# Maximum pass of attention as 64-row matmul pairs on the two halves of TensorE's array, two pairs issued together

## Chip, cores and metric

The kernel runs on one core of a Trainium2 chip. The metric is the device time of one execution in microseconds (us): the median over runs. Engines are named as in the profile: PE (TensorE matmuls), PEld (its weight loads), DVE (VectorE), ACT (ScalarE), POOL (GpSimd) and SP (SyncE, which issues the transfers).

## What is computed

Four stages over x of 4 batches x 1024 positions x 256 features, each on the layer-normed x and added to it: a linear recurrent block, a sparse feed-forward block, attention, and the feed-forward block again. The change touches attention alone, where there are 8 heads of 64 and keys and values that come from one 64-wide latent:

```python
q = (x @ Wq.T).reshape(b, t, N_HEADS, HEAD_DIM)
kv_latent = x @ Wkv_down.T
k = (kv_latent @ Wk_up.T).reshape(b, t, N_HEADS, HEAD_DIM)
v = (kv_latent @ Wv_up.T).reshape(b, t, N_HEADS, HEAD_DIM)
scores = jnp.einsum('bqhd,bkhd->bhqk', q, k) * HEAD_DIM ** (-0.5)
attn = jax.nn.softmax(scores, axis=-1)
out = jnp.einsum('bhqk,bkhd->bqhd', attn, v)
return out.reshape(b, t, N_HEADS * HEAD_DIM) @ Wo.T
```

## The kernel before

The key projection is folded into the query, so that keys are the 64-wide latent for all heads. Work is split into 64 **items** W: batch B = W // 16, then head and half c of the 1024 queries, so an item is one head with 512 queries against 1024 keys. Numbers of 64 rows are kept as two f16 parts, high and low. In `kA` rows 0 to 63 hold the high part of the keys and rows 64 to 127 the low part, `qA` holds the high part of the queries in both halves of its rows, `kB` and `qB` the rest, so that two 128-row matmuls give an accurate score tile.

Each item has 8 **steps** kt, one for each 128 keys. On PE step kt of item W issues, in this order:

- at even steps a **pair of the maximum pass** for item W + 2, `max_scores(W + 2, j)` with j = kt / 2 (pairs 0 to 3): 128 of the item's 512 queries, taken with a stride of 4 (`every[:, j, :]`), against both halves of the keys, two matmuls of 128x512 (L1734) into the PSUM banks 2 (j % 2) and 2 (j % 2) + 1
- the **score tile** `scores(W, kt)`: two matmuls (L1746, L1748) into bank 6 or 7, which wait until ACT has done the exponential of the tile two before
- at steps 3, 4, 6 and 7 a quarter of `weighted(W - 1, .)`, 24 matmuls with 64 or 65 columns (L1763 to L1765)
- **side work** in two slots, the first at steps 0 and 1, the second at step 5: queries (L1673), keys (L1666), latent (L1680), transposes (L1659, L1689) and the output product (L1696) of this batch and its neighbours, by tables that name item and slot (`QUERY_AT`, `OUT_FINAL_AT` and others). All of it uses bank 4, and each piece first waits until the piece before has been read out of the bank.

DVE reduces each maximum pair (L1397, 128x1024 from two PSUM banks to one column). Pair j may be issued when the reduction of pair j - 2 is done, by `wait_from(pe, a_mx, W * MX + j - 1)`. DVE's queue holds, per item: reduction 0, low half of tile 0 (L1414), reduction 1, side work (L1381 is the low part of queries), reduction 2, low half of tile 4, reduction 3, and the division of the item before (L1406, L1408). POOL makes the low halves of the other six tiles (L673). ACT does for each tile the exponential (L1007) and, behind the next tile's exponential, its f16 high half (L1015), and copies of side work (L988, L993); DVE's and POOL's low halves wait for the high half. The four maxima go, scaled (L1000), by a small transfer of SP into a row of `qB`, long before the item's score tiles want them. Every engine's order is fixed by these loops.

Of the kernel before, what the change touches and what calls it, by code (L numbers as in the profile page):

```python
# [7 lines left out]
F16 = mybir.dt.float16  # L8
BF16 = mybir.dt.bfloat16
ALU = mybir.AluOpType  # L10
ACT = mybir.ActivationFunctionType
X = mybir.AxisListType.X

P = 128
# [3 lines left out]
CH = 512  # L18
# [6 lines left out]
HD = 64  # L25
# [20 lines left out]
def hybrid_block_kernel(nc, x_in, W_in, b_in, params_log, W_mid, b_mid, w1_w, w1_b, w2_w, w2_b,  # L46
# [4 lines left out]
    with ctx:  # L51
# [3 lines left out]
        def sem(name):  # L55
            return ctx.enter_context(nc.semaphore(name))
# [47 lines left out]
        def carve(shape, dt=F32, parts=P):  # L104
            n = 1
            for s in shape:
                n *= s
            words = n if dt == F32 else (n + 1) // 2
            a = arena[0:parts, room[0]:room[0] + words]
            room[0] += words  # L110
            assert room[0] <= ARENA, room[0]
            if dt != F32:
                a = a.bitcast(dt)
            if len(shape) == 2:
                a = a.rearrange("p (a b) -> p a b", a=shape[0])
            if len(shape) == 3:
                a = a.rearrange("p (a b c) -> p a b c", a=shape[0], b=shape[1])
            return a
# [71 lines left out]
        kB_words = arena[:, room[0]:room[0] + TIME]  # L190
        kB = [carve([TIME], F16) for _ in range(2)]
        kA = [carve([TIME], F16) for _ in range(2)]
        latR = [carve([TIME // P, HD + 1], F16) for _ in range(2)]
        latL = [carve([TIME // P, HD], F16) for _ in range(2)]
        mx = [carve([TPC]) for _ in range(2)]
# [26 lines left out]
        ps = [psum[:, i, :] for i in range(8)]  # L222
# [78 lines left out]
        a_k = sem("a_key_high")  # L301
# [35 lines left out]
        ALL = BATCH * ITEMS  # L337
# [28 lines left out]
        def place(W):  # L366

            B, w = W // ITEMS, W % ITEMS
            hh, c = w // 2, w % 2
            return B, hh, c, hh % Q_RING  # L370

        def query_done(W):

            B, hh, c, slot = place(W)
            return ((B * GROUPS + hh // 2) * 2 + c) * 2 + hh % 2 + 1
# [15 lines left out]
        def wait_from(engine, sem_, value):  # L391

            if value > 0:
                engine.wait_ge(sem_, value)
# [319 lines left out]
        def _(act):  # L714
# [258 lines left out]
            def keys(B, c, bank):  # L973
                cs = slice(c * CH, c * CH + CH)
                act.wait_ge(a_kps, B * 2 + c + 1)
                nc.scalar.activation(kA[B % 2][:, cs], ps[bank][:, :], ACT.Copy).then_inc(a_k, 1)
                nc.scalar.activation(kB[B % 2][0:HD, cs], ps[bank][0:HD, :], ACT.Copy).then_inc(a_k, 1)

            def latent(B, c, bank):
                act.wait_ge(a_lps, B * 2 + c + 1)  # L980
# [41 lines left out]
            for c in range(2):  # L1022
                keys(0, c, 4 + c)
# [8 lines left out]
            for W in range(ALL):  # L1032
                B, w = W // ITEMS, W % ITEMS
# [426 lines left out]
        def _(pe):  # L1460
            mm = nc.tensor.matmul
# [83 lines left out]
            for a in range(NH // 2):  # L1545
                o = bank_for(4 + a)
                for k in range(KB2):
                    last = nc.tensor.transpose(o[:, k * P:k * P + P], wo_n[:, k, a * P:a * P + P], ident[:, :])
                last.then_inc(s_pe0, 1)
            for a in range(NH // 2):  # L1550
                o = bank_for(8 + a)
                pe.wait_ge(s_ev0, 5 + a)
                for r in (0, HD):
                    last = mm(o[r:r + HD, 0:D], wv_n[r:r + HD, a, :], woT[r:r + HD, a, :], start=True, stop=True)
                last.then_inc(s_pe0, 1)
            for k in range(KB2):
                for odd in range(2):
                    o = bank_for(12 + 2 * k + odd)
                    for a in range(NH // 2):
                        rows = slice(HD * odd, HD * odd + HD)  # L1560
                        last = mm(o[:, a * HD:a * HD + HD], wq_n[rows, a, k * P:k * P + P], wk_n[rows, a, :],
                                  start=True, stop=True)
# [162 lines left out]
            def max_scores(W, j):  # L1725

                B, hh, c, slot = place(W)
                if j == 0:
                    pe.wait_ge(a_kl, B * 2 + 2)
                    pe.wait_ge(a_dup, query_done(W))  # L1730
                wait_from(pe, a_mx, W * MX + j - 1)
                every = qA[:, slot, c * CH:c * CH + CH].rearrange("p (q j) -> p j q", j=TPC)
                for half in range(2):
                    last = mm(ps[2 * (j % 2) + half][:, :], every[:, j, :],  # L1734
                              kA[B % 2][:, half * CH:half * CH + CH], start=True, stop=True)
                last.then_inc(a_mps, 1)

            def scores(W, kt):

                B, hh, c, slot = place(W)  # L1740
                if kt == 0:
                    pe.wait_ge(a_qm, 16 * (W + 1))
                    pe.wait_ge(a_ql, query_done(W))
                wait_from(pe, a_P, W * KT + kt - 1)
                o = ps[6 + kt % 2]
                mm(o[:, :], kA[B % 2][:, kt * P:kt * P + P], qA[:, slot, c * CH:c * CH + CH],  # L1746
                   start=True, stop=False)
                mm(o[:, :], kB[B % 2][:, kt * P:kt * P + P], qB[:, slot, c * CH:c * CH + CH],  # L1748
                   start=False, stop=True).then_inc(a_sps, 1)

            def weighted(W, j):


                B, c = W // ITEMS, W % 2
                if j == 0:
                    pe.wait_ge(a_ll, B * 2 + 2)
                    wait_from(pe, a_O, W * 2)
                    pe.wait_ge(a_lD, low_done(W, LOW_DVE[-1]))
                    pe.wait_ge(a_lP, low_done(W, LOW_POOL[-1]))
                o = ps[5][:, j * (HD + 1):(j + 1) * (HD + 1)]  # L1760
                js = slice(j * P, j * P + P)
                for kt in range(KT):
                    mm(o, pr_hi[c][:, kt, js], latR[B % 2][:, kt, :], start=kt == 0, stop=False)  # L1763
                    mm(o[:, 0:HD], pr_hi[c][:, kt, js], latL[B % 2][:, kt, :], start=False, stop=False)  # L1764
                    last = mm(o, pr_lo[c][:, kt, js], latR[B % 2][:, kt, :], start=False, stop=kt == KT - 1)  # L1765
                if j == TPC - 1:
                    last.then_inc(a_ops, 1)
# [13 lines left out]
            for j in range(2):  # L1781
                max_scores(0, j)
# [3 lines left out]
            for j in range(2, TPC):  # L1786
                max_scores(0, j)
            for j in range(TPC):
                max_scores(1, j)
# [3 lines left out]

            for W in range(ALL):
                for kt in range(KT):
                    if kt % 2 == 0 and W + 2 < ALL:
                        max_scores(W + 2, kt // 2)
                    scores(W, kt)
                    if kt in WEIGHTED_AT and W:
                        weighted(W - 1, WEIGHTED_AT[kt])  # L1800
                    if kt < 2:
                        slot_work(W, 0, kt)
                    if kt == 5:
                        slot_work(W, 1, 0)
                        slot_work(W, 1, 1)
# [42 lines left out]
```

## Time and profile before

| | |
|---|---|
| median of 3 runs | 1529.7 us (1526.95 to 1532.33) |
| the profiled execution's own time | 1530.73 us |
| its span | 1529.0 us |
| busy in the span | PE 1276.4, DVE 1179.4, ACT 1122.6, POOL 1032.6 us |
| attention loop, about 561 to 1245 us | 684 us |
| mean granted clock over the span | 0.946 |

Busy time counts a matmul from its start to its modelled end, so matmuls that follow each other overlap: one of 512 f16 columns lasts 0.38 us, and the next starts 0.22 us behind it. On ACT and DVE too an instruction starts somewhat before the one ahead has ended. Where an engine is full is better read from starts than from busy shares.

### The profile page before, as it was taken

What the parts mean: (1) busy time and instruction counts of PE and PEld (TensorE: products, weight loads), DVE (VectorE), ACT (ScalarE), POOL (GpSimd) and SP (SyncE); (2) the same over time, 40 slices, a digit from 0 to 9 for tenths busy, and PEclk for the clock granted to TensorE, in tenths of its full rate; (3) what the DMA queues carried; (4) which work ended last, traced back from release to release, by engine and by line L of the source; (5) the groups of instructions that cost most, each with busy time, mean ns of one, the idle gap of its engine ahead of it and who ended that gap; (6) DMA issues with size and microseconds to landing.
All of it is one profiled execution on the core that took longest, in us unless ns stands there. A gap on an engine that the chain in (4) does not pass through costs nothing.

```text
span 1529.0 us, 32894 instructions
## 1 busy us (share of the span) xinstructions
PE 1276.4 (83%) x10332; PEld 782.4 (51%) x10332; DVE 1179.4 (77%) x2871; ACT 1122.6 (73%) x2453; POOL 1032.6 (68%) x1169
## 2 busy tenths in 40 slices
PE   5879998877666678999999999999999999777765
PEld 2435444444343444555566566665666557344433
DVE  7989888369999957776767667776677663699997
ACT  3424342577777749997988988888888895788885
POOL 3477886338888837776767667676676772188887
PEclk9989999979989889999999999999999999899997
DMA  6000000000000000000000000000000000000000
GB/s 193 30 1 1 0 0 0 1 1 0 0 0 0 0 1 2 2 2 2 2 2 2 2 2 2 2 2 1 2 2 2 2 2 1 0 14 27 14 27 27
DMA packets 26242, 14.32 MB, mean 9 GB/s; under 512 B 14406, under 2 KB 25868, under 8 KB 26124
## 3 DMA queue, kind: packets, MB, share of 16 engines
q1 hardware_dynamic: 26124, 12.74, 3.1%
q8 instruction: 75, 1.23, 0.3%
q14 instruction: 43, 0.35, 0.1%
HBM read 8.47 MB, written 4.19 MB: 8 GB/s over the span
## 4 chain that ended last, share of the span: by engine, by line
PE 38%; DVE 20%; issue 18%; POOL 11%; ACT 11%; DVEq 2%; ACTq 0%; DMA 0%; SPq 0%; POOLq 0%
POOL arena L673 5%; PE banks L1734 5%; PE banks L1746 4%; PE banks L1748 4%; DVE arena L1292 4%; DVE arena L1287 4%; PE banks L1673 4%; PE banks L1696 3%; ACT arena L1007 3%; DVE arena L1194 3%; PE banks L1763 3%; PE banks L1765 2%; PE banks L1764 2%; ACT arena L1015 2%; PE banks L1624 2%
## 5 line engine op out<-in xcount | busy, mean ns | idle before, releaser
L673 POOL TENSOR_TENSOR arena<-arena 128x512 f16<-128x512 f32 x384 | 440.4, 1163 | 206.0 <-ACT arena L1015 203.6
L1007 ACT ACTIVATE arena<-banks 128x512 f32<-128x512 f32 x512 | 304.1, 599 | 82.8 <-PE banks L1748 77.6
L1015 ACT ACTIVATE arena<-arena 128x512 f16<-128x512 f32 x512 | 316.1, 631 | 0.1
L1397 DVE TENSOR_REDUCE arena<-banks 128x1 f32<-128x1024 f32 x256 | 309.5, 1216 | 4.4 <-PE banks L1734 2.0
L1763 PE MATMUL banks<-arena 128*128 128x65 f16 x2048 | 213.9, 195 | 12.9 <-POOL arena L673 12.9
L1763 PEld LDWEIGHTS banks<-arena 128*128 128x128 f16 x2048 | 190.1, 97 | 50.4 <-issue 23.1
L1414 DVE TENSOR_TENSOR arena<-arena 128x512 f16<-128x512 f32 x128 | 102.1, 798 | 147.5 <-ACT arena L1015 147.5
L1764 PE MATMUL banks<-arena 128*128 128x64 f16 x2048 | 214.1, 192 | 0.0
L1765 PE MATMUL banks<-arena 128*128 128x65 f16 x2048 | 213.3, 193 | 0.0
L1292 DVE MATCH_REPLACE8 arena<-arena 128x256 f32<-128x256 f32 x512 | 205.1, 407 | 0.4 <-issue 0.4
L1287 DVE MAX8 arena<-arena 128x8 f32<-128x256 f32 x512 | 189.9, 411 | 17.8 <-ACT arena L850 13.1
L1764 PEld LDWEIGHTS banks<-arena 128*128 128x128 f16 x2048 | 189.7, 99 | 27.2
L1746 PE MATMUL banks<-arena 128*128 128x512 f16 x512 | 194.6, 380 | 7.3 <-ACT arena L1007 7.1
L1748 PE MATMUL banks<-arena 128*128 128x512 f16 x512 | 194.0, 379 | 0.0
L1765 PEld LDWEIGHTS banks<-arena 128*128 128x128 f16 x2048 | 189.9, 96 | 0.0
L1734 PE MATMUL banks<-arena 128*128 128x512 f16 x512 | 152.6, 380 | 3.4 <-DVE arena L1397 3.4
L1610 PE MATMUL banks<-fW,arena 128*128 128x256 f32 x256 | 86.0, 466 | 43.2 <-ACT arena L894 43.2
L1606 PE MATMUL banks<-ident,arena 128*128 128x128 f32 x128 | 27.8, 302 | 67.0 <-POOL arena L616 67.0
L860 ACT ACTIVATE arena<-arena 128x256 f32<-128x256 f32 x128 | 63.9, 500 | 26.5 <-DVE arena L1294 26.4
L1610 PEld LDWEIGHTS banks<-fW,arena 128*128 128x128 f32 x256 | 49.9, 216 | 64.7 <-ACT arena L894 59.5
L1597 PE MATMUL banks<-fW,arena 128*128 128x256 f32 x256 | 82.3, 454 | 0.0
L1746 PEld LDWEIGHTS banks<-arena 128*128 128x128 f16 x512 | 50.2, 98 | 61.4 <-ACT arena L1007 24.0
(203 smaller groups left out, 2819.9 us busy)
## 6 DMA issues: line engine op xcount, KB each, us to landing
x<-in_L_attn_a_x SPq DMA_DIRECT2D x8, 512.0 KB, 3.9
out<-x SPq DMA_DIRECT2D x8, 512.0 KB, 2.9
arena<-arena SPq DMA_DIRECT2D x64, 1.0 KB, 1.9
arena<-in_L_attn_a_W_in SPq DMA_DIRECT2D x1, 768.0 KB, 5.9
arena<-in_L_attn_a_W_mid SPq DMA_DIRECT2D x1, 512.0 KB, 6.8
arena<-in_L_attn_a_w_w SPq DMA_DIRECT2D x2, 256.0 KB, 6.9
arena<-in_L_attn_b_Wq SPq DMA_DIRECT2D x1, 512.0 KB
arena<-in_L_attn_b_Wo SPq DMA_DIRECT2D x1, 512.0 KB
```

What stands on the lines that cost most here:

```text
L673: nc.gpsimd.tensor_tensor(pr_lo[c][:, kt, :], pr[:, kt, :], pr_hi[c][:, kt, :], ALU.subtract).then_inc(a_lP, 1)
L1007: nc.scalar.activation(pr[:, kt, :], ps[6 + kt % 2][:, :], ACT.Exp, scale=SM_SCALE).then_inc(a_P, 1)
L1015: nc.scalar.activation(pr_hi[c][:, kt, :], pr[:, kt, :], ACT.Copy).then_inc(a_hi, 1)
L1287: nc.vector.max(m8[p][:, i, r, :], src).then_inc(f_k[i], 1)
L1292: nc.vector.match_replace(wk[p][:, i, r % 2, :], m8[p][:, i, r, :], src, TAKEN).then_inc(f_k[i], 1)
L1397: nc.vector.tensor_reduce(mx[c][:, j:j + 1], psum[:, 2 * pair:2 * pair + 2, :].rearrange("p a b -> p (a b)"), X, ALU.max).then_inc(a_mx, 1)
L1734: last = mm(ps[2 * (j % 2) + half][:, :], every[:, j, :], kA[B % 2][:, half * CH:half * CH + CH], start=True, stop=True)
L1746: mm(o[:, :], kA[B % 2][:, kt * P:kt * P + P], qA[:, slot, c * CH:c * CH + CH], start=True, stop=False)
L1748: mm(o[:, :], kB[B % 2][:, kt * P:kt * P + P], qB[:, slot, c * CH:c * CH + CH], start=False, stop=True).then_inc(a_sps, 1)
L1763: mm(o, pr_hi[c][:, kt, js], latR[B % 2][:, kt, :], start=kt == 0, stop=False)
L1764: mm(o[:, 0:HD], pr_hi[c][:, kt, js], latL[B % 2][:, kt, :], start=False, stop=False)
L1765: last = mm(o, pr_lo[c][:, kt, js], latR[B % 2][:, kt, :], start=False, stop=kt == KT - 1)
```

## The change

The maximum pass uses the high part of the keys alone, 64 rows instead of 128. The first 512 keys are read from rows 0 to 63 of `kA`; a new tile `kM` holds the high part of the last 512 keys in rows 64 to 127, written by one more copy of ACT per batch. The two matmuls of a pair so stand on the upper and the lower half of the array's rows and write different banks. The maxima are only the shift of the exponentials. And the pairs are issued two together, at steps 0 and 4, instead of one at each even step.

```diff
+        kM = [carve([CH], F16) for _ in range(2)]
...
                 nc.scalar.activation(kA[B % 2][:, cs], ps[bank][:, :], ACT.Copy).then_inc(a_k, 1)
-                nc.scalar.activation(kB[B % 2][0:HD, cs], ps[bank][0:HD, :], ACT.Copy).then_inc(a_k, 1)
+                last = nc.scalar.activation(kB[B % 2][0:HD, cs], ps[bank][0:HD, :], ACT.Copy)
+                if c:
+                    last = nc.scalar.activation(kM[B % 2][HD:P, :], ps[bank][HD:P, :], ACT.Copy)
+                last.then_inc(a_k, 1)
...
-                for half in range(2):
-                    last = mm(ps[2 * (j % 2) + half][:, :], every[:, j, :],
-                              kA[B % 2][:, half * CH:half * CH + CH], start=True, stop=True)
+                for half, k_half in enumerate((kA[B % 2][0:HD, 0:CH], kM[B % 2][HD:P, :])):
+                    last = mm(ps[2 * (j % 2) + half][:, :], every[HD * half:HD * half + HD, j, :], k_half,
+                              start=True, stop=True)
                 last.then_inc(a_mps, 1)
...
                 for kt in range(KT):
-                    if kt % 2 == 0 and W + 2 < ALL:
-                        max_scores(W + 2, kt // 2)
+                    if kt % 4 == 0 and W + 2 < ALL:
+                        for j in range(2):
+                            max_scores(W + 2, kt // 2 + j)
                     scores(W, kt)
```

PE, item 18, from the last weighted product of the item before through steps 0 to 3, before (L1734 is the maximum pair, L1746 and L1748 a score tile, L1696 side work):

```order
L1765 MATMUL banks<-arena 128x65
L1734 MATMUL banks<-arena 128x512 x2
L1746 MATMUL banks<-arena 128x512
L1748 MATMUL banks<-arena 128x512
L1696 MATMUL banks<-voB,arena 128x256 x2
L1746 MATMUL banks<-arena 128x512
L1748 MATMUL banks<-arena 128x512
L1696 MATMUL banks<-voB,arena 128x256 x2
L1734 MATMUL banks<-arena 128x512 x2
L1746 MATMUL banks<-arena 128x512
L1748 MATMUL banks<-arena 128x512
```

The same place in the changed kernel (the lines are 4 further on: L1738 is the pair, L1750 and L1752 the score tile, L1700 the side work):

```order
L1769 MATMUL banks<-arena 128x65
L1738 MATMUL banks<-arena 128x512 x4
L1750 MATMUL banks<-arena 128x512
L1752 MATMUL banks<-arena 128x512
L1700 MATMUL banks<-voB,arena 128x256 x2
L1750 MATMUL banks<-arena 128x512
L1752 MATMUL banks<-arena 128x512
L1700 MATMUL banks<-voB,arena 128x256 x2
L1750 MATMUL banks<-arena 128x512
L1752 MATMUL banks<-arena 128x512
```

Pair 1 has moved from behind the side work to the front of score tile 0, and tile 2 follows tile 1 and the side work alone.

PE, item 18, step 6, before:

```order
L1765 MATMUL banks<-arena 128x65
L1746 MATMUL banks<-arena 128x512
L1748 MATMUL banks<-arena 128x512
L1689 MATMUL banks<-ident,xcT 128x128 x4
L1734 MATMUL banks<-arena 128x512 x2
L1746 MATMUL banks<-arena 128x512
L1748 MATMUL banks<-arena 128x512
L1763 MATMUL banks<-arena 128x65
```

and changed, where pair 3 now stands with pair 2 ahead of score tile 4 (first five rows) and no longer ahead of tile 6 (last rows):

```order
L1769 MATMUL banks<-arena 128x65
L1738 MATMUL banks<-arena 128x512 x4
L1750 MATMUL banks<-arena 128x512
L1752 MATMUL banks<-arena 128x512
L1767 MATMUL banks<-arena 128x65
...
L1693 MATMUL banks<-ident,xcT 128x128 x4
L1750 MATMUL banks<-arena 128x512
L1752 MATMUL banks<-arena 128x512
L1767 MATMUL banks<-arena 128x65
```

Pair 3 has gone two steps forward. DVE's queue, here from reduction 0 of such an item, reads the same before and after but for line numbers (before is shown, with the semaphores that each row waits for):

```order
L1397 TENSOR_REDUCE arena<-banks 128x1 [waits a_max_scaled,a_max_psum]
L1414 TENSOR_TENSOR arena<-arena 128x512 [waits a_exp_high]
L1397 TENSOR_REDUCE arena<-banks 128x1 [waits a_max_psum]
L1381 TENSOR_TENSOR arena<-banks,arena 64x512 [waits a_query_high] x2
L1397 TENSOR_REDUCE arena<-banks 128x1 [waits a_max_psum]
L1414 TENSOR_TENSOR arena<-arena 128x512 [waits a_exp_high]
L1397 TENSOR_REDUCE arena<-banks 128x1 [waits a_max_psum]
```

Nothing on it moved: reductions 1 and 3 stand behind a low half (L1414) that waits for ACT.

## Rows read from the trace of the kernel before

**Rows 1.** Busy time by stretch: the attention loop

```profile
core 0: us, PE busy (x) PEld busy (x) DVE busy (x) ACT busy (x) POOL busy (x), PEclk, DMA share, GB/s
561.00:1245.00 684.00, 641.49 (x7875) 413.60 (x7875) 489.31 (x635) 595.14 (x1186) 477.18 (x449) 1.00 0.01 2
```

**Rows 2.** Costliest groups of the page: busy us, mean ns, idle before

```profile
L1007 ACT ACTIVATE arena<-banks 128x512 f32<-128x512 f32 x512 | 304.1, 599 | 82.8 <-PE banks L1748 77.6
```

**Rows 3.** Timeline of PE, item 18: start us, duration us, line

```profile
761.01 0.38 PE L1746 MATMUL banks<-arena 128*128 128x512 f16 x1
...
761.45 1.03 PE L1696 MATMUL banks<-voB,arena 128*128 128x256 f32 x4
762.31 0.38 PE L1746 MATMUL banks<-arena 128*128 128x512 f16 x1
...
765.63 0.60 PE L1734 MATMUL banks<-arena 128*128 128x512 f16 x2
766.07 0.38 PE L1746 MATMUL banks<-arena 128*128 128x512 f16 x1
...
767.24 0.38 PE L1746 MATMUL banks<-arena 128*128 128x512 f16 x1
...
767.67 0.60 PE L1689 MATMUL banks<-ident,xcT 128*128 128x128 f32 x4
...
771.30 0.38 PE L1746 MATMUL banks<-arena 128*128 128x512 f16 x1
```

**Rows 4.** Timeline of DVE, item 18: low halves and reductions 1 and 3

```profile
764.15 0.75 DVE L1414 TENSOR_TENSOR arena<-arena 128x512 f16<-128x512 f32 x1 [1.60 <-ACT arena L1015]
764.82 1.21 DVE L1397 TENSOR_REDUCE arena<-banks 128x1 f32<-128x1024 f32 x1
...
769.07 0.86 DVE L1414 TENSOR_TENSOR arena<-arena 128x512 f16<-128x512 f32 x1 [1.58 <-ACT arena L1015]
769.86 1.21 DVE L1397 TENSOR_REDUCE arena<-banks 128x1 f32<-128x1024 f32 x1
```

**Rows 5.** Timelines of DVE and PE, items 20 and 21

```profile
788.53 0.69 DVE L1381 TENSOR_TENSOR arena<-banks,arena 64x512 f16<-64x512 f32 x1 [0.94 <-ACT arena L988]
...
790.91 0.74 DVE L1414 TENSOR_TENSOR arena<-arena 128x512 f16<-128x512 f32 x1 [0.43 <-ACT arena L1015]
...
781.59 0.38 PE L1746 MATMUL banks<-arena 128*128 128x512 f16 x1
...
789.28 1.99 PE L1696 MATMUL banks<-voB,arena 128*128 128x256 f32 x8 [0.89 <-DVE arena L1381]
...
794.31 0.38 PE L1746 MATMUL banks<-arena 128*128 128x512 f16 x1
...
805.70 0.38 PE L1746 MATMUL banks<-arena 128*128 128x512 f16 x1
```

**Rows 6.** Timeline of PE, first score tiles of items 57 and 58

```profile
1201.05 0.38 PE L1746 MATMUL banks<-arena 128*128 128x512 f16 x1
...
1211.65 0.38 PE L1746 MATMUL banks<-arena 128*128 128x512 f16 x1
```

**Rows 7.** Timelines of PE and DVE, item 59 (no side work)

```profile
1226.27 0.38 PE L1746 MATMUL banks<-arena 128*128 128x512 f16 x1
...
1231.07 0.38 PE L1746 MATMUL banks<-arena 128*128 128x512 f16 x1
...
1225.43 2.34 DVE L1397 TENSOR_REDUCE arena<-banks 128x1 f32<-128x1024 f32 x2
...
1229.89 1.22 DVE L1397 TENSOR_REDUCE arena<-banks 128x1 f32<-128x1024 f32 x1
```

**Rows 8.** Timeline of PE ahead of the loop: a pair that waits for a reduction

```profile
566.60 0.62 PE L1734 MATMUL banks<-arena 128*128 128x512 f16 x2 [0.45 <-DVE arena L1397]
```

**Rows 9.** Timeline of PE, setup: whole array, then 64 rows

```profile
41.41 0.38 PE L1541 MATMUL banks<-ident,xcT 128*128 128x128 f32 x2
41.72 0.34 PE L1544 MATMUL banks<-ident,arena 64*128 64x64 f32 x2
...
44.42 1.95 PE L1554 MATMUL banks<-arena 64*64 64x256 f32 x16
```

## Prediction

> **What bounds the kernel now.** I read the busy time by stretch first, then the costliest groups, then one attention item in the timeline. The attention loop takes 684 of the 1529.0 us, at the full granted clock (1.00, which is the 2.4 GHz level), with PE busy 641 us, ACT 595, DVE 489 and POOL 477 [rows 1]. The reader is to see there that PE and ACT are both near the bound, and in the costliest groups that ACT stands idle behind PE's score tiles for 77.6 us, ahead of its 512 exponentials of 0.60 us [rows 2]. So PE is the engine to relieve. Item 18 of the 64 shows how: PE has no idle stretch between its first score tile at 761.01 and the next item's at 771.30, 10.29 us [rows 3]. A pair of maximum matmuls holds PE for 0.43 us of it (765.63 to 766.07), so the maximum pass is 4 x 0.43 = 1.73 us of PE per item.
>
> What sets when a pair may start is DVE: each pair writes the two banks that the pair two before it left for the reduction L1397. In this order that hardly ever binds, and rows 3 and 4 show why: the reduction of pair 1 ends at 766.03 and pair 3 comes to PE only behind the score tile of 767.24. There is more than 1 us to spare. The same for the last reduction: it ends at 771.07, and the pair that needs its banks comes two steps into the next item.
>
> DVE's queue is the part that the change does not touch. It reads: reduction, low half (L1414), reduction, reduction, low half, reduction. Each low half waits for ACT [rows 4], which waits for a score tile. Reduction 1 starts at 764.82 right behind the low half of 764.15, and the one of pair 3 at 769.86 behind that of 769.07. Neither waits for its own pair, so issuing pairs 1 and 3 earlier makes neither reduction earlier.
>
> **The change part by part.** Removed: nothing in count; PE still issues eight 512-column matmuls per item. What changes is that two of them may run at once. The nearest rows are the setup's 64x64 products L1554: 16 in 1.95 us [rows 9], at most 0.12 us each, against (1.99 - 1.03) / 4 = 0.24 for the same 256 columns on the whole array (L1696 x8 and x4) [rows 3, 5]. Two of these run side by side. They use opposite column halves too, which the new pairs do not, so the bounds for a new pair are 0.22 us (full overlap) and 0.43 (none). I take 0.22.
>
> Added: two changes of the array's shape around each group of two pairs. Two transposes on the whole array start 0.11 apart ((0.60 of four - 0.38 of two) / 2 [rows 3, 9]), so the second L1541 starts at 41.52, and L1544, the first on half the rows, waits for no semaphore and starts at 41.72 [rows 9]: 0.20 behind, 0.09 more than its place. The first weights after a break are not loaded ahead: 0.62 us for a pair against 0.59 to 0.60 [rows 3, 8], 0.03. I take 0.12 for a change of shape. Bounds: 0 (the gap was something else) and 0.28 (a matmul's whole tail, 0.38 - 0.22 = 0.16, and 0.12 of weight load, about L1541's 0.11 spacing). The Trainium skill, "TensorEngine Tiling (Array Packing)", Key Properties, has the rule that speaks against this change: switching the tiling mode drains TensorE. It gives no price; the row's 0.09 is what it would be here, and without the rule the term would be 0.
>
> PE's own sum: 1.73 becomes 4 x 0.22 + 4 x 0.12 = 1.36 us, 0.37 less per item, 0.25 more at each group where 0.43 less stands two steps later.
>
> Moved: pair 1 from step 2 to step 0, pair 3 from step 6 to step 4. Behind each stand all of PE's later instructions, first the score tile that ACT wants. Pair 3 now needs reduction 1 at once. In item 18 score tile 1 starts at 762.31 and reduction 1 ends at 764.82 + 1.21 = 766.03, 3.72 later. Then the release to PE (0.06: L1381 ends at 789.22, L1696 starts at 789.28 [rows 5]), the pair 0.22 and the change back 0.12: score tile 4 comes 4.12 after score tile 1, where it came 3.76 after. PE by itself would be there at 3.76 - 0.43 + 0.25 = 3.58, so it stands still for half a microsecond. In the same way, from score tile 5 (767.24) to the end of reduction 3 (771.07) is 3.83, and the next item's first tile comes 4.23 after instead of 4.06. Together 0.53 longer. The spacing from low half to reduction is 0.67 in one place and 0.79 in the other [rows 4]; with both near 0.67 it is 0.42. I take 0.46.
>
> By kinds of item (62 issue maximum pairs; the counts are those of the tables of side work, and lengths are read between first score tiles):
> - 16 items with both slots filled and no query, as item 18: +0.46 each, +7.4 us.
> - 11 with a query, or latent work after one, and a long second slot. As in item 20, PE stands before that slot until DVE's L1381 is done (0.89 of idle time), so the wait at step 4 is hidden. The evacuation chain starts 0.43 earlier because the pair ahead of score tile 2 is gone. The pair behind the slot is gone too, and the next group is 0.25 longer: -0.61 each, -6.7.
> - Behind a query, DVE's last chain: its low half at 790.91 comes 0.43 earlier, then 0.67 + 1.21 + 0.06 + 0.34 gives 792.76, which is 11.2 after 781.59 [rows 5]. Nine such items with a short second slot take 11.39 now (794.31 to 805.70): -0.2 each, -1.8. Five with an empty one take 10.60 (1201.05 to 1211.65) [rows 6]: +0.6, +3.0.
> - 8 light items. In item 59 reduction 1 ends at 1226.64, so score tile 4 comes at 1227.04 instead of 1226.27 (+0.77). Reduction 3 ends at 1231.11; 1.17 after step 4 stands score tile 5, 1227.44, so 3.67 + 0.40 = 4.07 replaces 3.63 (to 1231.07) [rows 7]: +1.2. The heavier ones of the eight have about +0.3; the mean is taken as 0.85, +6.8.
> - The 13 that are left (transposes, keys, the first items) have partly one, partly the other: an estimate of +0.3, +3.9.
>
> Sum: +12.6. The new copy of ACT (64x512, once per batch, about 0.6 us by the 512-column exponential [rows 2], beside PE's work) adds at most 2 us; I take 0.4. That is +13.0. The profiled execution took 1530.7, 1.0 above the median, so 1543.7 there and 1543 for the median: slower by 0.9%.
>
> The Trainium skill says on the same page, PSUM Bottleneck, that tiling speeds TensorE but not the evacuation of PSUM. The 1.21 us rows of L1397 beside a 0.43 us pair agree.
>
> **The rivals.**
> - PE's saving comes through: 62 x 0.37 = 23 us, 1507. This is the other side. Its mechanism is that ACT gets score tile 4 in time because DVE's gate does not bind. It needs reduction 1 to end by the time that PE reaches pair 3, half a microsecond earlier than the rows show, and nothing on DVE or in front of it is moved. 12%.
> - A change of shape costs nothing: then every gated step is 0.12 shorter, 42 items x 0.24, nine x 0.12 and eleven x 0.25, -14: 1529. Against it stands the 0.09 of rows 9, one place only. 7%. The Trainium skill, "TensorE: Matmul & The Clock Gate", Part 3 (measured speedup vs the span model), lets packed tiles end about 4 ns apart and names no cost of entering, so by it the time is this one.
> - The halves don't run at once (both matmuls write all 128 partitions, which L1554 did not). Each pair keeps its 0.43: gated steps +0.22 each, 42 x 0.43, nine x 0.22 and eleven x 0.43, +25: 1568. 14%.
> - The change of shape costs 0.28: +0.16 on each gated step, +18: 1561. 12%.
> - The terms cancel within the measurement: the light and the plain items lose little because ACT, with more idle time, delivers sooner. Between 1525 and 1534. 7%.
> - My forecast, about 1535 to 1555: 48%.
>
> **How the numbers follow.** A difference under 0.3% (4.6 us) can't be told from none. Faster 0.12, same 0.14 (the free change and the cancelling), slower 0.74. The range goes from 1526 (most of the free change of shape) to 1568 (no overlap); what lies outside is the PE-bound case and both bad prices together.
>
> **What would show it.** Right: L1738 pairs whose second matmul starts within 0.02 us of the first; in most items PE idle before the second pair of a group, released by L1401; the interval from score tile 1 to 4 near 4.1 us; ACT's idle time behind PE longer, though PE's work is shorter; query items with long slots near 12.1 us. Wrong: plain items near 9.9 us, no wait on L1401 at the groups, starts 0.22 apart inside a pair, or a gap above 0.2 us between the last pair and the score tile behind it.

## The result: 1544.6 us, 0.94% slower

The changed kernel takes 1544.55 us (median of 4 runs, 1543.63 to 1545.48) against 1529.75 (4 runs of the kernel before, 1526.95 to 1532.33): ratio 1.0094, 95% interval 1.0081 to 1.0108. Its profiled execution took 1545.48 us, its span is 1543.8, 14.8 us more than the 1529.0 of before. From the first maximum pair to the last score tile it is 720.5 us (558.30 to 1278.82) against 705.4 (558.86 to 1264.21), so all of it lies in attention.

The page of the changed kernel: first the sums by engine, then from the costliest groups the exponential, DVE's reduction and the maximum pair.

```profile
PE 1271.9 (82%) x10332; PEld 759.8 (49%) x10332; DVE 1166.9 (76%) x2871; ACT 1129.8 (73%) x2457; POOL 1031.1 (67%) x1169
...
L1011 ACT ACTIVATE arena<-banks 128x512 f32<-128x512 f32 x512 | 303.7, 597 | 91.7 <-PE banks L1752 81.4
...
L1401 DVE TENSOR_REDUCE arena<-banks 128x1 f32<-128x1024 f32 x256 | 309.5, 1216 | 1.4
...
L1738 PE MATMUL banks<-arena 64*128 64x512 f16 x512 | 101.8, 407 | 39.0 <-DVE arena L1401 34.8
```

The maximum pass has lost a third of its busy time on PE (101.8 us, 152.6 before), since the two of a pair are busy over each other. Each of its matmuls is a little longer (407 ns, 385 for a score tile's first), but that is no price of the overlap: in the first experiment below the second pair of a group, overlapped too, has 0.38 us a matmul, and the 0.40 us ones stand right behind a change of shape. In exchange 34.8 us of waiting for DVE's reduction stand before it; before it was 3.4. ACT, the engine that PE's saving should have fed, stands idle a little longer, 91.7 us instead of 82.8 [rows 2].

The waits by line in 561 to 1261 us show the same for the weight loads and for the matmuls of the pairs (what waits, for what: us in total, times, longest). The second row is idle time of the matmuls. The first row is not all loss, since the matmuls ahead are still running in part of it.

```profile
PEld banks L1738 <- DVE arena L1401: 69.6, 110, 1.8
...
PE banks L1738 <- DVE arena L1401: 34.8, 84, 1.6
```

Item 18, PE, from its first score tile (start, length, engine, line, operation, shapes, in brackets the idle time and what ended it):

```profile
773.29 0.39 PE L1750 MATMUL banks<-arena 128*128 128x512 f16 x1
...
774.59 0.38 PE L1750 MATMUL banks<-arena 128*128 128x512 f16 x1
...
777.45 0.19 PE L1769 MATMUL banks<-arena 128*128 128x65 f16 x1
777.58 0.41 PE L1738 MATMUL banks<-arena 64*128 64x512 f16 x2
778.32 0.41 PE L1738 MATMUL banks<-arena 64*128 64x512 f16 x2 [0.33 <-DVE arena L1401]
778.66 0.39 PE L1750 MATMUL banks<-arena 128*128 128x512 f16 x1
...
779.83 0.38 PE L1750 MATMUL banks<-arena 128*128 128x512 f16 x1
...
783.13 0.83 PE L1738 MATMUL banks<-arena 64*128 64x512 f16 x4
783.90 0.39 PE L1750 MATMUL banks<-arena 128*128 128x512 f16 x1
```

and DVE over the same time:

```profile
776.43 0.69 DVE L1418 TENSOR_TENSOR arena<-arena 128x512 f16<-128x512 f32 x1 [1.86 <-ACT arena L1019]
777.04 1.22 DVE L1401 TENSOR_REDUCE arena<-banks 128x1 f32<-128x1024 f32 x1
...
781.68 0.69 DVE L1418 TENSOR_TENSOR arena<-arena 128x512 f16<-128x512 f32 x1 [1.96 <-ACT arena L1019]
782.28 1.22 DVE L1401 TENSOR_REDUCE arena<-banks 128x1 f32<-128x1024 f32 x1
```

The reader is to see one gate, twice per item. Pair 2 runs at 777.58. Pair 3 needs the banks of pair 1, whose reduction ends at 777.04 + 1.22 = 778.26; it starts at 778.32, and score tile 4 behind it at 778.66. That reduction started late only because it stands in DVE's queue behind the low half of 776.43, which waited 1.86 us for ACT. From score tile 1 to tile 4 it is 4.07 us, where it was 3.76 [rows 3]. The second reduction ends at 783.50, and the next item's first tile comes at 783.90. The item takes 10.61 us, was 10.29. Two matmuls of a pair in 0.41 us, one alone being 0.40, means starts about a hundredth of a microsecond apart: the halves of the array do run at once.

### The profile page after: what moved, and what is told of

It reads as the page before. It is cut to its first block, busy times and chain, and to the rows that moved or that the text cites. A ratio compares the mean times of both kernels' runs of the same rounds, so it can differ in the third digit from the quotient of the medians.

```text
span 1543.8 us, 32898 instructions
## 1 busy us (share of the span) xinstructions
PE 1271.9 (82%) x10332; PEld 759.8 (49%) x10332; DVE 1166.9 (76%) x2871; ACT 1129.8 (73%) x2457; POOL 1031.1 (67%) x1169
## 4 chain that ended last, share of the span: by engine, by line
PE 27%; DVE 25%; issue 20%; ACT 17%; POOL 8%; DVEq 2%; ACTq 0%; DMA 0%; SPq 0%; POOLq 0%
ACT arena L1019 6%; ACT arena L1011 5%; DVE arena L1296 4%; DVE arena L1401 4%; DVE arena L1291 4%; PE banks L1750 3%; PE banks L1677 3%; PE banks L1752 3%; DVE arena L1198 3%; POOL arena L674 3%; PE banks L1738 2%; DVE arena L1418 2%; PE banks L1700 2%; PE banks L1628 2%; ACT arena L992 2%
## 5 line engine op out<-in xcount | busy, mean ns | idle before, releaser
L1011 ACT ACTIVATE arena<-banks 128x512 f32<-128x512 f32 x512 | 303.7, 597 | 91.7 <-PE banks L1752 81.4
L1418 DVE TENSOR_TENSOR arena<-arena 128x512 f16<-128x512 f32 x128 | 95.8, 748 | 188.0 <-ACT arena L1019 188.0
L1750 PE MATMUL banks<-arena 128*128 128x512 f16 x512 | 197.0, 385 | 7.7 <-ACT arena L1011 7.7
L1752 PE MATMUL banks<-arena 128*128 128x512 f16 x512 | 195.1, 381 | 0.0
L1738 PE MATMUL banks<-arena 64*128 64x512 f16 x512 | 101.8, 407 | 39.0 <-DVE arena L1401 34.8
L1750 PEld LDWEIGHTS banks<-arena 128*128 128x128 f16 x512 | 50.5, 99 | 82.9 <-issue 41.0
```

The source lines that it names most:

```text
L1011: nc.scalar.activation(pr[:, kt, :], ps[6 + kt % 2][:, :], ACT.Exp, scale=SM_SCALE).then_inc(a_P, 1)
```

## The experiments

Times are medians with their lowest and highest run, ratios are to the kernel before with 95% intervals. "The attention stretch" is first maximum pair to last score tile: 705.4 us before, 720.5 changed; it ends at 1264.21 before, later than the 1245 of rows 1. It is given because the stages ahead of attention, which no kernel here touches, ended up to 4 us apart in the profiles (first pair between 554.80 and 558.86).

### DVE's queue follows PE's order

```diff
-                    if kt % 2 == 0 and W + 2 < ALL:
-                        largest_of(W + 2, kt // 2)
+                    if kt % 4 == 0 and W + 2 < ALL:
+                        for j in range(2):
+                            largest_of(W + 2, kt // 2 + j)
```

> The changed kernel with one more edit: DVE's queue takes reductions 0 and 1 together at step 0 and 2 and 3 together at step 4, each ahead of the low half of that step. My theory (reductions 1 and 3 stood behind a low half that waits for ACT, and so held the second pair of each group): the waits of the pairs on DVE go from 104 us to under 15 us, plain items such as item 18 go from 10.61 to about 9.9 us, below the 10.29 of before, and the time to about 1508 us (1500 to 1518). Rival (the change of the array's shape and the 64-row form are what costs, DVE's wait only fills time that PE would lose anyway): the time stays within 5 us of 1544. Second rival (ACT takes over as the bound): 1520 to 1530.

Measured: 1514.44 us (1513.22 to 1515.56), ratio 0.9894 (0.9877 to 0.9910), attention stretch 691.4. One edit on DVE turns 0.94% slower into 1.06% faster. In the waits by line, 561 to 1261 us again, the pairs' waits for DVE are nearly gone:

```profile
PEld banks L1739 <- DVE arena L1401: 4.7, 6, 1.0
PE banks L1739 <- DVE arena L1401: 4.1, 6, 1.6
```

DVE now does both reductions ahead of each low half, here behind item 19's first score tile:

```profile
772.51 2.35 DVE L1401 TENSOR_REDUCE arena<-banks 128x1 f32<-128x1024 f32 x2
775.54 0.69 DVE L1418 TENSOR_TENSOR arena<-arena 128x512 f16<-128x512 f32 x1 [0.69 <-ACT arena L1019]
...
777.14 2.35 DVE L1401 TENSOR_REDUCE arena<-banks 128x1 f32<-128x1024 f32 x2 [0.58 <-PE banks L1739]
```

and PE finds the banks free, four matmuls in a row and the score tile 0.56 us behind the first:

```profile
772.40 0.39 PE L1751 MATMUL banks<-arena 128*128 128x512 f16 x1
...
776.69 0.62 PE L1739 MATMUL banks<-arena 64*128 64x512 f16 x4
777.25 0.39 PE L1751 MATMUL banks<-arena 128*128 128x512 f16 x1
...
782.28 0.39 PE L1751 MATMUL banks<-arena 128*128 128x512 f16 x1
```

Item 19 takes 9.88 us, which is 10.29 less PE's own saving of 0.37 to 0.41. Item 18, which the expectation names, takes 10.09 and so gains half of that. This is the rival "PE's saving comes through", reached by another order of DVE. It misses the expected 1508 by 6 us: items in which something else was already last gained less (item 4 takes 10.39 where 10.60 was), the first two items take 23.5 us instead of 21.2, and item 2 takes 11.51 instead of 9.66, with a granted clock of 0.93 in 590 to 600 us where it was 1.00.

### Reordering DVE alone, in the kernel before

The edit of DVE's queue as above, and nothing else of the change.

> The kernel before (128-row pairs, one at each even step) with DVE's reductions two together ahead of the low halves: the control for the reordering of DVE. Reduction 1 then waits for a pair that comes at step 2, and the low half of tile 0 stands behind it. My theory: nothing gained, 1528 to 1536, since no pair waits for DVE in the kernel before. Rival (the DVE order is better by itself, and that is the 30 us): under 1520.

Measured: 1529.49 us (1526.77 to 1530.70, 10 runs), ratio 1.0000 (0.9989 to 1.0010). The order of DVE is worth nothing by itself. It pays only where PE's pairs are issued in twos: 30 us with 64-row pairs, and 24 with 128-row ones (1547.11 to 1522.70, both below).

### Only the first of the two gates undone

```diff
-                    if kt % 2 == 0 and W + 2 < ALL:
-                        largest_of(W + 2, kt // 2)
+                    if kt in (0, 4, 6) and W + 2 < ALL:
+                        for j in {0: (0, 1), 4: (2,), 6: (3,)}[kt]:
+                            largest_of(W + 2, j)
```

> The changed kernel with only reduction 1 moved ahead of the low half of tile 0; reduction 3 stays behind the low half of tile 4. It tells the two gates apart. My theory: score tile 1 to 4 goes from about 4.06 to 3.5 us in plain items, and the next item's first tile stays gated; items with a query gain nothing, since what is won before the second slot is waited out there. About 1530 us (1526 to 1536), about half of the 30 us between the changed kernel and the one with both moved. Rival (the first gate alone holds everything): 1514 to 1518; (the second alone): 1542 or more.

Measured: 1526.47 us (1524.98 to 1528.51), ratio 0.9978 (0.9968 to 0.9987). Item 18, PE:

```profile
773.20 0.62 PE L1739 MATMUL banks<-arena 64*128 64x512 f16 x4
773.76 0.39 PE L1751 MATMUL banks<-arena 128*128 128x512 f16 x1
...
778.23 0.83 PE L1739 MATMUL banks<-arena 64*128 64x512 f16 x4
```

The group at step 4 is now tight (0.62 us for four), the one at the next item's step 0 still holds the wait (0.83, as at 783.13 above). From score tile 1 at 770.22 to tile 4 at 773.76 is 3.54 us. Undone in this order, reduction 1 behind the low half costs 18 us of the 30 and reduction 3 the other 12.

### Split without grouping

The changed kernel with PE's pairs issued one at each even step again:

```diff
-                    if kt % 4 == 0 and W + 2 < ALL:
-                        for j in range(2):
-                            max_scores(W + 2, kt // 2 + j)
+                    if kt % 2 == 0 and W + 2 < ALL:
+                        max_scores(W + 2, kt // 2)
```

> The changed kernel with its pairs put back one by one at the even steps: the 64-row form alone. Each of the four pairs then pays its own two changes of shape, about 0.10 us going in and 0.12 coming out by the trace of the changed kernel, and saves 0.22 by its overlap, and no reduction is late. My theory: within 4 us of the kernel before, about 1531. Rival (the 64-row form costs more than it shows between matmuls): 1540 or more.

Measured: 1538.44 us (1537.28 to 1541.20), ratio 1.0057 (1.0041 to 1.0074); attention stretch 713.3, 7.9 more than before. It misses the expected 1531 by 7 us. Item 18 is near the 10.29 of before, 10.34 us: four pairs, each with two changes of shape, save nothing. Most of the 8 us are elsewhere. Three items that make the next batch's keys, as item 28, take 12.89 us, were 12.12; and the first two items take 22.5 us, were 21.2. In item 28 the new copy (L980) stands on ACT ahead of an exponential that no longer waits for PE:

```profile
878.63 0.59 ACT L977 ACTIVATE arena<-banks 128x512 f16<-128x512 f32 x1
879.11 0.58 ACT L978 ACTIVATE arena<-banks 64x512 f16<-64x512 f32 x1
879.70 0.59 ACT L980 ACTIVATE arena<-banks 64x512 f16<-64x512 f32 x1
880.32 0.60 ACT L1011 ACTIVATE arena<-banks 128x512 f32<-128x512 f32 x1
```

Together these two kinds are 3 x 0.77 + 1.3 = 3.6 of the 7.9 us. Item 45 is another 1.6 (15.93, was 14.31): the granted clock is 0.84 in 1077 to 1082 us of this profile. The other 58 items add 2.7, most of them 0.05 each. In the changed kernel, item 28 takes 12.00 us, and with 128-row pairs in the same order and no copy (next section) 12.01; the copy costs at most the 0.2 us that other items gain between these two.

### Grouping without the split

The kernel before, its 128-row pairs issued two together:

```diff
-                    if kt % 2 == 0 and W + 2 < ALL:
-                        max_scores(W + 2, kt // 2)
+                    if kt % 4 == 0 and W + 2 < ALL:
+                        for j in range(2):
+                            max_scores(W + 2, kt // 2 + j)
```

> The kernel before with its 128-row pairs issued two together at steps 0 and 4, nothing else: the move alone. My theory (the move makes the second pair wait for DVE): slower than the changed kernel, since the pair behind the gate takes 0.43 us instead of 0.22 + 0.12: about 1553 us (1546 to 1560), and pairs wait for DVE about as long as in the changed kernel. Rival (the loss came with the 64-row form): about 1530.

Measured: 1547.11 us (1545.81 to 1548.99), ratio 1.0114 (1.0097 to 1.0131), inside the expected range and 6 us under its middle; its waits:

```profile
PEld banks L1734 <- DVE arena L1397: 79.2, 110, 1.9
...
PE banks L1734 <- DVE arena L1397: 26.8, 80, 1.4
```

They are nearly those of the changed kernel (79.2 and 26.8 us beside 69.6 and 34.8), with no 64-row matmul in attention. The gate comes of the grouping alone. The split on top of it is worth 2.6 us by the medians (1544.55 against 1547.11) and 3.8 by the two profiles (attention stretch 724.3 and 720.5). The second has two parts: from item 2 on the items take 8.3 us less with the split (item 18, 10.61 where 10.83), and items 0 and 1 take 4.5 more (27.0 where 22.5), of which more under "The start at full clock".

With DVE's queue in the new order as well:

> The kernel before with 128-row pairs two together at steps 0 and 4 and with DVE's reductions two together ahead of the low halves: move and DVE order without the 64-row form. My theory: PE's work is that of before and nothing is gated: about 1530 (1525 to 1536), and its distance to the same order with the 64-row form (about 22 us) is what the overlap is worth. Rival (the grouping itself saves or costs time): more than 8 us from 1530.

Measured: 1522.70 us (1521.87 to 1525.60), ratio 0.9956 (0.9940 to 0.9973), attention stretch 700.2. I had expected no gain, and missed by 7 us. Items as 18 stay at 10.29; the items with a query gain (12.29 where 12.73 was, 10.95 where 11.39 was), 0.44 or one pair. The prediction has this effect in its query items and puts it down to the pair ahead of score tile 2, which is no longer in front of what their evacuation chain waits for; no run here takes that apart. So part of what the whole gives with DVE reordered (15 us) is the grouping (7), and the split adds 8.3, not the 23 that 62 x 0.37 promised.

### Both matmuls of a pair on the same half

The reordered kernel of the first experiment, with the second matmul on rows 0 to 63 too, so that the two can't overlap:

```diff
-                for half, k_half in enumerate((kA[B % 2][0:HD, 0:CH], kM[B % 2][HD:P, :])):
-                    last = mm(ps[2 * (j % 2) + half][:, :], every[HD * half:HD * half + HD, j, :], k_half,
-                              start=True, stop=True)
+                for half in range(2):
+                    last = mm(ps[2 * (j % 2) + half][:, :], every[0:HD, j, :],
+                              kA[B % 2][0:HD, half * CH:half * CH + CH], start=True, stop=True)
```

> The kernel with 64-row pairs two together and DVE's reductions two together (1514.4 us), but with both matmuls of a pair on rows 0 to 63 of the array, so that they can't run at once; the maxima are the same, and the copy into kM is still made. If the overlap is what PE gains: pairs 0.22 apart inside again, a group 0.43 us longer, both groups exposed in plain items (9.88 to about 10.7 us), one of them hidden in items with a query: about 1550 us (1543 to 1560). Rival (PE's relief came from the regrouping alone, the overlap is hidden behind ACT): 1514 to 1522.

Measured: 1546.05 us (1544.41 to 1547.56), ratio 1.0107 (1.0088 to 1.0127).

```profile
772.79 1.05 PE L1739 MATMUL banks<-arena 64*128 64x512 f16 x4
773.78 0.39 PE L1751 MATMUL banks<-arena 128*128 128x512 f16 x1
```

Four matmuls now take 1.05 us instead of 0.62, and the score tile comes 0.99 behind the first instead of 0.56. The overlap is worth 0.43 per group and 31.6 us in the whole (1546.05 - 1514.44). Against the same order with 128 rows (1522.70) the 64-row form without overlap loses 23 us: half the rows are no cheaper (item 18, 10.74 where 10.30), and the changes of shape are paid on top. 4.1 of the 23 us are items 0 and 1 (26.0 where 21.9), and 1.9 the three items with the copy (12.20 where 11.57).

### Another place for DVE's low halves

The gate could also be opened by giving DVE the low halves of tiles 2 and 6 instead of 0 and 4, so that reductions 1 and 3 come first:

```diff
-        LOW_DVE, LOW_POOL = (0, 4), (1, 2, 3, 5, 6, 7)
+        LOW_DVE, LOW_POOL = (2, 6), (0, 1, 3, 4, 5, 7)
```

> The changed kernel with DVE making the low halves of tiles 2 and 6 instead of 0 and 4, POOL those of 0 and 4: a second way to put reductions 1 and 3 ahead of a low half that waits, which leaves the place of every reduction in the step loop. My theory (the wait of the reductions behind the low half is the whole gate): waits of pairs on DVE fall below 25 us and the time to 1510 to 1522. Rival (what helped was that reductions stand two together, or that they stand at steps 0 and 4): above 1535.

Measured: 1567.89 us (1567.14 to 1568.94), ratio 1.0249 (1.0230 to 1.0268). Expected was a gain; this is the slowest kernel of the study. The pairs' waits did fall, from 69.6 and 34.8 us to 23.4 and 13.7, but other waits grew. Item 24, first two rows DVE, last row PE:

```profile
846.76 1.05 DVE L1418 TENSOR_TENSOR arena<-arena 128x512 f16<-128x512 f32 x1 [1.61 <-ACT arena L1019]
847.73 1.40 DVE L1385 TENSOR_TENSOR arena<-banks,arena 64x512 f16<-64x512 f32 x2
```

```profile
849.18 1.99 PE L1700 MATMUL banks<-voB,arena 128*128 128x256 f32 x8 [1.72 <-DVE arena L1385]
```

L1385, which frees the side work's bank, now stands behind the low half of tile 2, and PE waits 1.72 us before its second slot. The item takes 13.14 us, and the same kind takes 12.09 in the changed kernel. Most of the loss is in six other items, those with the next batch's keys and first queries (12, 13, 28, 29, 44 and 45): they hold 22.5 of the 24.0 us by which the items grew in sum, item 28 takes 15.35 us where 12.00 was, and through item 29 (902.4 to 920.6 us) the granted clock is 0.81, where the changed kernel has 1.00. Which wait ends last in them was not followed. The stall was moved, not removed.

### The start at full clock

In the changed kernel the granted clock falls where attention begins. The busy time by stretch of before, then of the changed kernel (sum, PE, PEld, DVE, ACT and POOL busy, granted clock, DMA share, GB/s):

```profile
565.00:575.00 10.00, 7.38 (x27) 2.84 (x28) 8.61 (x9) 2.76 (x6) 0.00 (x0) 1.00 0.01 0
575.00:590.00 15.00, 11.37 (x104) 5.63 (x103) 10.59 (x13) 14.41 (x30) 12.30 (x11) 1.00 0.01 1
```

```profile
565.00:575.00 10.00, 7.31 (x19) 2.38 (x18) 6.52 (x6) 1.17 (x3) 0.00 (x0) 0.52 0.01 0
575.00:590.00 15.00, 11.28 (x33) 3.58 (x32) 8.03 (x9) 10.50 (x21) 8.39 (x8) 0.75 0.01 0
```

Ahead of the first score tile PE has only maximum pairs and stands behind DVE's reductions between them. With 128-row pairs the clock stays at its 2.4 GHz level, with 64-row pairs it goes to the 1.2 GHz one, and a pair takes longer and the items' other work too:

```profile
568.19 0.62 PE L1738 MATMUL banks<-arena 64*128 64x512 f16 x2 [0.52 <-DVE arena L1401]
...
571.00 0.61 PE L1750 MATMUL banks<-arena 128*128 128x512 f16 x1
```

Items 0 and 1 take 27.0 us (571.00 to 598.04), before 21.2 (570.52 to 591.73). The next kernel is the changed one, with the pairs of items 0 and 1, all issued before the loop, in the old form:

```diff
+                    if W < 2:
+                        last = mm(ps[2 * (j % 2) + half][:, :], every[:, j, :],
+                                  kA[B % 2][:, half * CH:half * CH + CH], start=True, stop=True)
+                    else:
...
```

> The changed kernel with the maximum pairs of items 0 and 1 alone in the 128-row form, the other 62 items in the 64-row form. In all kernels with 64-row pairs ahead of the loop the granted clock is 0.50 in the 5 us ahead of it, where PE is paced by reductions, and mixed until about 590 us; in the kernels with 128-row pairs it is 1.00 there, and the first two items take 22.5 us (move alone) instead of 27.0. If the shorter PE work ahead of the loop is what lets the clock fall: 1.00 in 565 to 575 us, items 0 and 1 in about 22.5 us, and the time 4 to 5 us less, about 1540. Rival (the clock there hangs on something else, the 64-row form itself in the loop): no change, 1544 to 1545.

Measured: 1539.20 us (1537.16 to 1541.34), ratio 1.0055 (1.0036 to 1.0074).

```profile
565.00:575.00 10.00, 6.87 (x27) 2.40 (x26) 6.72 (x8) 5.14 (x11) 1.99 (x2) 1.00 0.00 0
575.00:590.00 15.00, 11.91 (x104) 5.75 (x105) 9.11 (x11) 11.88 (x24) 9.70 (x10) 0.89 0.02 1
```

The first stretch is back at 1.00. The first two items take 24.0 us, 3.1 less, and the attention stretch is 3.4 shorter (717.1); the other 2 of the 5.3 us between the medians lie ahead of attention in the profile and can't be put down to the edit. So about half of the 5.8 us that these items had lost came back with the clock of the start. In the rest are the gate, which holds here too (at 573.24 the second pair of a group still stands 1.00 us behind DVE), and a low stretch around 580 us that remains (0.89 above). That one is not a matter of the 64-row form: the kernel with 128-row pairs and both orders has one too, 0.66 in 575 to 580 us.

At the start the form decides. In 565 to 570 us all seven kernels with 64-row pairs ahead of the loop have 0.50 to 0.59, all six with 128-row pairs there 1.00. The expectation above puts it down to PE's shorter work. The same-half kernel speaks against that, for its two matmuls run one after the other and hold PE as long as 128-row ones. Its pairs, and its clock:

```profile
560.36 1.05 PE L1739 MATMUL banks<-arena 64*128 64x512 f16 x4
562.59 0.59 PE L1739 MATMUL banks<-arena 64*128 64x512 f16 x2 [1.17 <-DVE arena L1401]
...
565.00:575.00 10.00, 9.50 (x21) 2.74 (x20) 6.34 (x6) 2.17 (x4) 0.00 (x0) 0.58 0.01 0
```

and the same pairs of the kernel before, which keeps 1.00:

```profile
563.24 1.03 PE L1734 MATMUL banks<-arena 128*128 128x512 f16 x4
565.56 0.60 PE L1734 MATMUL banks<-arena 128*128 128x512 f16 x2 [1.29 <-DVE arena L1397]
```

So what tells them apart is the 64-row form of the matmuls and not that PE is done sooner; why the form does it, no run shows.

### The copy of the keys on POOL, and the best version

In the reordered kernel the copy into `kM` is taken from ACT and made by POOL out of `kA`:

```diff
+            def move_keys(B):
+                pool.wait_ge(a_k, (B * 2 + 1) * 2 + 2)
+                nc.gpsimd.tensor_scalar(kM[B % 2][HD:P, :], kA[B % 2][0:HD, CH:TIME], 1.0, 0.0,
+                                        ALU.mult, ALU.add).then_inc(a_km, 1)
...
-                if c:
-                    last = nc.scalar.activation(kM[B % 2][HD:P, :], ps[bank][HD:P, :], ACT.Copy)
...
```

> The 1514.4 us kernel with the copy into kM taken from ACT, where it stands ahead of an exponential and ahead of the signal to DVE, and given to POOL, from kA. By item 12 of a batch, which lost 0.4 us against the kernel with 128-row pairs in the same order (12.00 against 11.58), and the first items: 2 us less, 1512 to 1513. Rival (the copy is hidden on ACT): no difference, 1514 to 1515. Should POOL's wait bind: 1516 or more.

Measured: 1513.78 us (1511.18 to 1515.80), ratio 0.9888 (0.9867 to 0.9908). Item 28 falls from 12.00 to 11.37, but the whole (attention stretch 691.4 in both) can't be told from the 1514.44 without it. The three items of this kind give 1.9 us together, and in the profile item 58 takes 1.5 of it back, 11.99 where 10.49 was: the granted clock falls there to 0.66 in 1198 to 1203 us, 1.00 in the kernel without the edit.

```profile
1198.00:1203.00 5.00, 4.69 (x57) 2.91 (x58) 2.35 (x2) 1.51 (x4) 2.68 (x4) 0.66 0.03 3
```

Why the clock falls there, and whether it does in every execution, is not shown.

With the old form for items 0 and 1 as well:

> The kernel with 64-row pairs and reductions two together, kM copied by POOL (1513.8 us), and with items 0 and 1 in the 128-row form. By the same reasoning the first two items go from 23.7 to about 22 us: 1511 to 1513. Rival (clock not set by that): 1514.

Measured: 1510.69 us (1508.32 to 1512.70), ratio 0.9864 (0.9848 to 0.9881), attention stretch 688.7, the first two items 21.4 us (23.7 without it). Item 58 takes 11.99 us here too. It is the fastest of all, 1.4% under the kernel before.

## Why the prediction was right, and where its sizes were off

The forecast was 1543, measured is 1544.55, and the mechanism is the one it named. By its own steps:

- **The pair.** Full overlap, 0.22 us each, was right (0.41 us for both with their tails; the same-half experiment puts 0.43 on each group of two pairs). The rival "halves don't run at once" is out. (Two small slips in the pair of before: 766.07 - 765.63 is 0.44, and 4 x 0.43 is 1.72; nothing hangs on them.)
- **The change of shape**, taken as 0.12. Into it: the last weighted product starts at 777.45 and the pair at 777.58, 0.13 instead of the 0.03 between ordinary weighted products, so 0.10 more. Out of it: 0.34 from the last pair to the score tile, 0.22 of it the pair, so 0.12. Both rivals on it, 0 and 0.28, are out. The Trainium skill, "TensorEngine Tiling (Array Packing)", Key Properties, says that switching the tiling mode drains TensorE, and the trace agrees in that both changes cost time, 0.10 and 0.12 us. Whether the array is then empty it can't show, since the ends of matmuls are modelled (the pair's at 778.73, behind the score tile's start at 778.66).
- **The gate.** Score tile 1 to 4: 4.07 us against 4.12 foretold. Score tile 5 to the next item: 783.90 - 779.83 = 4.07 against 4.23 (it was 4.06 before). The mis-sized term is the spacing from low half to reduction, taken as 0.67 and 0.79: it is 0.61 and 0.60. The low half is shorter here (0.69 us; 0.75 and 0.86 before [rows 4]), and I took its length over from rows of before without a reason that it should stay. So the 16 plain items lost 6.0 us, not 7.4.
- **Query items.** Item 20 takes 12.09 us (794.51 to 806.60), foretold 12.1; item 21, 11.18, foretold 11.2; item 57, 11.18 where 10.60 was, foretold 11.2. The classes sum to -7.7, -1.9 and +2.9, foretold -6.7, -1.8 and +3.0. Item 59 takes 9.97 (1234.04 to 1244.01), foretold 8.76 + 1.2, and the eight light items sum to +6.4, foretold +6.8.

```profile
794.51 0.39 PE L1750 MATMUL banks<-arena 128*128 128x512 f16 x1
...
806.60 0.39 PE L1750 MATMUL banks<-arena 128*128 128x512 f16 x1
...
817.78 0.39 PE L1750 MATMUL banks<-arena 128*128 128x512 f16 x1
```

- **The 13 others**, an estimate of +3.9: measured +8.0, of which items 0 and 1 alone are +5.8. Here the prediction lacked a thing altogether: that 64-row pairs, where DVE sets the pace, would bring the clock down. That this error and the one on plain items have opposite signs is chance, and the sum (+13.7 against +13.0) looks better for it than its terms are. It also leaves out 1.0 us between the first pair and the first score tile and 0.4 in item 62, where the grouping without the split has 1.1 and 0.4 as well; with them it is the 15.1 us of the attention stretch.
- **The copy into kM**, 0.4 us in all, is about right for the changed kernel (item 28: 12.00 with it, 12.01 in the same order without, where others gain 0.2; three such items). Where ACT is what is waited for it costs its whole 0.6 or more: 12.12 to 12.89 in the split without grouping, and 12.00 to 11.37 when POOL takes it over in the reordered kernel. No run shows it in the total.
- **The rivals.** "PE's saving comes through" at 1507 had its condition put exactly: reduction 1 must end before PE reaches pair 3. The reordered kernel meets it and takes 1514; the change as made does not.

The costs and gains apart, each as the difference of two medians: the gate costs 30 us (1544.55 to 1514.44), the overlap saves 32 (1546.05 to 1514.44), and the grouping with its fitting order of DVE saves 7 (1529.86 to 1522.70). The split adds only 8.3 us to the grouping (8.8 by the profiles) where PE's own sum says 23. By items: eleven gain 0.42 each, as from both groups, 39 only 0.21, as from one, and items 59 and 60 0.3 together, 13.0 in all; the three items with the copy lose 1.3, and items 0 to 2 lose 2.9. Not settled: what hides the other group in the 39 items.

## What to carry to other kernels

Who issues work earlier on one engine must look at the queue of the engine that frees its buffers: with PE's pairs in twos, the same six instructions of DVE in another order were worth 30 us, and in the old order of PE nothing. Before moving an instruction to open a gate, ask what stands behind it in its new place; the low halves of tiles 2 and 6 opened this gate and closed another, 23 us net the wrong way. In this kernel half-array matmuls pay through overlap alone, and each group of them pays about 0.22 us for entering and leaving, so they are worth grouping.

## What the chip showed that I had not expected

64-row matmuls, where DVE sets the pace, made the clock slower: with the same waits behind DVE, the granted clock in 565 to 575 us is 0.52 with 64-row pairs and 1.00 with 128-row ones. It is 0.58 with 64-row matmuls that run one after the other and hold PE as long as the 128-row ones, so the shorter work is not what did it. The low level lasted into items that had full work (score tile matmuls of 0.61 us instead of 0.38 at 571.00, and 0.75 as the mean of 575 to 590). And two matmuls on different rows, both writing all 128 partitions of their own bank, share the output side without loss: 0.41 us for both.
